# Linear phase: the sums of q's squares beside those of u, and one product of v between the turned scales and their spreading

## The reference

```python
x = x + attention(layernorm(x), wq, wk, wv, wo)
x = x + ffn(layernorm(x), W_r, W_k, W_v, mu_r, mu_k)
x = x + linear(layernorm(x), Wq, Wk, Wv, Wf, Wb, A_log, dt_bias, Wg, bg, Wo, norm_w)
x = x + ffn(layernorm(x), W_r, W_k, W_v, mu_r, mu_k)        # x: (2, 2048, 128) float32

def linear(x, ...):                                        # 16 heads of width 64
    q, k, v = silu(x @ Wq), silu(x @ Wk), silu(x @ Wv)     # each (2, 2048, 16, 64)
    f = sigmoid(x @ Wf - dt_bias);  beta = sigmoid(x @ Wb)
    q, k = l2norm(q), l2norm(k)                            # over the 64 of a head
    for t in tokens:                                       # state: (2, 16, 64, 64)
        o[t] = (q[t] . state) * f[t]
        state = A[head] * state + beta[t] * outer(k[t], v[t])
    o = o * rsqrt(mean(o * o, over the 64) + 1e-5) * norm_w
    return (o * sigmoid(x @ Wg + bg)) @ Wo
```

## Time and profile before

| what | value |
|---|---|
| median of 3 runs | 908.69 us (906.55 to 910.41) |
| the profiled execution | 905.67 us, its span 901.5 us |
| PE busy, share of the span | 814.4 us, 90% |
| DVE, ACT, POOL busy | 556.2, 570.5, 584.7 us (62%, 63%, 65%) |
| mean granted clock of TensorE | 0.981; 1.00 in all of the steps of the linear phase that are read below |
| transfers | 12 GB/s of HBM over the span |

### The profile page before, as it was taken

The page is one execution under the profiler, slowest core; times in us unless marked ns, Lnnn a source line. Parts: engine busy times, 40 slices in busy tenths (PEclk is TensorE's granted clock), DMA queues, the critical chain, the costliest instruction groups (busy, mean ns, idle before and its releaser), DMA issues.

```text
span 901.5 us, 31429 instructions
## 1 busy us (share of the span) xinstructions
PE 814.4 (90%) x13280; PEld 707.7 (79%) x13280; DVE 556.2 (62%) x1296; ACT 570.5 (63%) x1202; POOL 584.7 (65%) x514
## 2 busy tenths in 40 slices
PE   4958998999797799999999999999999999996977
PEld 3647997899696687888788888888888887875866
DVE  3976666566684356567467466567467566567463
ACT  4746554655565666767767767767767767664544
POOL 4983211320445888977977967977977977977332
PEclk9988999999998899999999999999999999999999
DMA  5101000100100000000000000000000000000011
GB/s 188 29 12 36 21 16 1 31 19 2 25 1 1 1 3 3 4 3 3 3 3 3 4 3 3 4 3 3 3 3 3 3 3 3 3 3 3 5 32 58
DMA packets 19417, 12.38 MB, mean 14 GB/s; under 512 B 7760, under 2 KB 18768, under 8 KB 19024
## 3 DMA queue, kind: packets, MB, share of 16 engines
q1 hardware_dynamic: 19280, 10.39, 4.0%
HBM read 8.29 MB, written 2.10 MB: 12 GB/s over the span
## 4 chain that ended last, share of the span: by engine, by line
PE 55%; POOL 4%; DVE 4%; issue 3%; ACT 2%; DVEq 0%; POOLq 0%; ACTq 0%
PE la_ps L1465 9%; PE la_ps L1467 8%; PE la_ps L1466 8%; PE la_o_ps L1528 4%; PE la_o_ps L1544 4%; PE la_s_ps L1558 3%; PE la_ps L1575 3%; PE la_ps L1509 3%; PE la_ps L1496 2%; PE la_ps L1609 2%; PE la_ps L1610 2%; PE la_ps L1611 2%; DVE la_u L1765 1%; POOL la_scale L2141 1%; PE la_ps L1598 1%
## 5 line engine op out<-in xcount | busy, mean ns | idle before, releaser
L2109 POOL TENSOR_TENSOR la_coef<-la_ssk,lt_mhalf 128x32 f32<-128x32 f32 x16 | 87.1, 5442 | 70.2 <-DVE la_ssk L1782 70.2
L1465 PE MATMUL la_ps<-la_x_hi,w_hi 128*128 128x256 f32 x384 | 115.0, 300 | 1.8 <-ACT la_v L1922 1.7
L1467 PE MATMUL la_ps<-la_x_hi,w_lo 128*128 128x256 f32 x384 | 107.5, 280 | 0.4 <-issue 0.4
L1466 PE MATMUL la_ps<-la_x_lo,w_hi 128*128 128x256 f32 x384 | 107.3, 279 | 0.0
L2141 POOL TENSOR_TENSOR la_scale<-la_scale,lt_mhalf 128x32 f32<-128x32 f32 x16 | 99.9, 6241 | 6.8 <-DVE la_scale L1758 6.8
L1805 DVE TENSOR_TENSOR lt_state<-la_s_ps,la_faded 128x512 f32<-128x512 f32 x62 | 42.6, 686 | 70.0 <-PE la_o_ps L1544 57.6
L1465 PEld LDWEIGHTS la_ps<-la_x_hi,w_hi 128*128 128x128 f32 x384 | 72.2, 188 | 11.2 <-issue 6.2
L713 ACT ACTIVATE at_probs<-at_s_ps,at_ntop 128x512 f32<-128x512 f32 (+2 forms) x80 | 49.0, 623 | 46.5 <-DVE at_ntop L655 46.4
L598 PE MATMUL at_o_ps<-V,at_probsT 128*128 128x128 f32 x544 | 74.5, 277 | 3.2 <-DVE at_probsT L507 2.0
L531 POOL CAST at_q_hi<-qk_hi 128x128 fp32r<-128x128 f32 x32 | 9.4, 294 | 104.6 <-PE at_s_ps L572 102.2
L598 PEld LDWEIGHTS at_o_ps<-V,at_probsT 128*128 128x128 f32 x544 | 68.9, 192 | 6.4 <-ACT at_probsT L729 2.3
(11 more groups left out here) (216 smaller groups left out, 2493.6 us busy)
## 6 DMA issues: line engine op xcount, KB each, us to landing
at_w_raw<-in_w SPq DMA_DIRECT2D x20, 128.0 KB, 2.2
X<-in_x SPq DMA_DIRECT2D x8, 256.0 KB, 2.9
out<-X SPq DMA_DIRECT2D x8, 256.0 KB, 2.3
qkv_cos<-in_cos SPq DMA_DIRECT2D x1, 1024.0 KB, 4.8
qkv_sin<-in_sin SPq DMA_DIRECT2D x1, 1024.0 KB, 6.9
lt_w_out<-in_w_out SPq DMA_DIRECT2D x4, 128.0 KB, 2.7
const<-in_const SPq DMA_DIRECT2D x1, 320.5 KB, 3.3
qkv_w<-in_w_qkv SPq DMA_DIRECT2D x1, 320.0 KB, 3.9
```

Of the source, the lines that this page charges most:

```text
L1465: eng.matmul(out, l_hi, r_hi, start=True, stop=False)
L1466: eng.matmul(out, l_hi, r_lo, start=False, stop=False)
L1467: return eng.matmul(out, l_lo, r_hi, start=False, stop=True)
L2109: eng.tensor_tensor(coef[:, :], ssk[:, :], mhalf[:, :], ALU.pow).then_inc(s["coef_step"], 1)
```

## The change

- `square_q` moves from ACT's first half of step m (two instructions of 1024 elements per partition) to the end of q's work in step m - 1, as one instruction of 2048 elements, into a buffer of its own, `la_sq_q`.
- PE sums q's squares directly behind those of u, ahead of `f2`, and no longer behind `k3`. The ring's list changes with it.
- DVE's `guard_q` stands between `add_totals` and `gather_totals`, no longer behind `new_state(m, 0, 0)`.
- `v2` stands on PE between `sB` and `b0`; on ACT its `silu` stands behind `copy_scales`, ahead of the second `square_k`.
- `la_total`, `la_scT` and `la_yT` now share one place in SBUF.

The diff, cut to its core:

```diff
...
         u = sb("u", [P, NP, W])
+        sq_q = sb("sq_q", [P, NP, W])
         with ExitStack() as before_scaling:
...
         ssq = sb("ssq", [P, W])
-        total = sb("total", [P, W])
+        with ExitStack() as before_scales:
+            total = before_scales.enter_context(nc.sbuf_tensor("la_total", [P, W], F32))
+        with ExitStack() as before_output:
+            scT = before_output.enter_context(nc.sbuf_tensor("la_scT", [P, W], F32R))
+        yT = sb("yT", [P, W])
         scale = sb("scale", [P, B, H])
-        scT = sb("scT", [P, W], F32R)
-        yT = sb("yT", [P, W])
...
         LAST = NT - 1
-        ring = Ring(("f0 f1 su f2 sT f3 be k0 k1 v0 v1 kT0 kT1 s10 s11 k2 k3 sq sB b0 b1 b2 b3 v2 v3 q0 q1 q2 q3 y g0 g1 yt g2 "
+        ring = Ring(("f0 f1 su sq f2 sT f3 be k0 k1 v0 v1 kT0 kT1 s10 s11 k2 k3 sB v2 b0 b1 b2 b3 v3 q0 q1 q2 q3 y g0 g1 yt g2 "
                      "kT2 kT3 s00 s01 g3 xt").split(), has, STEPS, BANKS)
...
                         eng.wait_ge(tables.ones_set, 10)
-                    eng.wait_ge(s["qsq_ready"], 2 * (m + 1))
+                    eng.wait_ge(s["qsq_ready"], m + 1)
                 else:
...
                         mm = eng.matmul(ps[bank][32 * quad:32 * (quad + 1), 0:W], pick[:, r if job == "sq" else 2 + r, :],
-                                        sq[:, chunk, :], start=(r == 0), stop=(r == 1))
+                                        (sq_q if job == "sq" else sq)[:, chunk, :], start=(r == 0), stop=(r == 1))
                 mm.then_inc(full[bank], 1)
...
                 if now:
+                    sum_squares(m, "sq")
                     by_feature(m, "f2")
...
                 if now:
-                    sum_squares(m, "sq")
                     recall(m, 0, 1)
...
                     turn_scales(m)
+                if nxt:
+                    by_token(m, "v2")
+                if prv:
                     for j in range(4):
...
                 if nxt:
-                    by_token(m, "v2")
                     by_token(m, "v3")
...
             def guard_q(m):
+                if m > 0:
+                    taken(eng, m, "su")
                 bank = written(eng, m, "sq")
...
                     add_totals(m)
+                if now:
+                    guard_q(m)
+                if prv:
                     gather_totals(m)
...
                     new_state(m, 0, 0)
-                    guard_q(m)
                 if nxt:
...
                     eng.wait_ge(s["qd_second"], m + 1)
-                    eng.wait_ge(s["qsq_ready"], 2 * (m + 1))
+                    eng.wait_ge(s["qsq_ready"], m + 1)
                 bank = written(eng, m, f"q{j}")
...
                 taken(eng, m, f"b{j}")
-                if j == 0 and exists(m):
-                    written(eng, m, "sq")
                 part = slice(2 * j, 2 * j + 2)
...
-            def square_q(m, half):
-                if half == 0 and m > 0:
-                    written(eng, m, "su")
-                part = slice(half * NP // 2, (half + 1) * NP // 2)
-                eng.activation(sq[:, part, :], qT[:, part, :], ACT.Square).then_inc(s["qsq_ready"], 1)
+            def square_q(n):
+
+                taken(eng, n - 1, "q3")
+                if n > 0:
+                    written(eng, n - 1, "sq")
+                eng.activation(sq_q[:, :, :], qT[:, :, :], ACT.Square).then_inc(s["qsq_ready"], 1)
...
                     written(eng, m, "y")
-                elif b == 0:
-                    written(eng, m, "sq")
                 eng.activation(sq[:, :, tile(b)], u[:, :, tile(b)], ACT.Square).then_inc(s["usq_ready"], 1)
...
                     silu_token(m, "k1")
-                if now:
-                    square_q(m, 0)
                 if nxt:
...
                     copy_kT(m, 1)
-                if now:
-                    square_q(m, 1)
                 if nxt:
...
                 if nxt:
+                    silu_token(m, "v2")
                     square_k(m + 1, 1)
...
                     high_u(m, 1)
-                if nxt:
-                    silu_token(m, "v2")
-                if prv:
                     high_u(m, 2)
...
                         silu_q(m, j)
+                    square_q(m + 1)
                 if m == -1:
```

## The result

The changed kernel takes 910.25 us (median of 20 runs, 907.92 to 914.56) against 906.70 us of the kernel before on the same chip (20 runs, 903.71 to 912.65). The ratio is 1.0033, with a 95% interval of 1.0017 to 1.0049: about 3.0 us slower (1.5 to 4.4). That is under the 0.5% (4.5 us) that the prediction took as the bound of a change, and in the range that was forecast, but more than the +0.4 us of the sum.

The account below looks back on a forecast made before the run. PE was taken to bound each step; terms -0.7 - 0.3 + 1.0 - 0.1 + 0.5 = +0.4 us, added to the median of 908.69, forecast 909.1 us, with an 8-in-10 range of 903.8 to 914.3 us.

Parts of the forecast that it names:

- its own case: Whole kernel: no change of size, chance 0.62, with its own range of 905.5 to 912 us.
- v2 in the gap: PE between `sB` and `b0`: filling the gap gains only 0.05 us a step, -0.7 us over 14 steps.
- The wait ahead of `y`: PE before `y`: a new wait for DVE's low part, 0.3 to 0.7 us a step.
- q's squares on ACT: ACT between q's `silu` and `copy_y`: one instruction of about 2.0 us, covered by the existing wait; cost 0.
- `sq` beside `su`: PE, q's sums beside u's: changeover saved, mostly given back waiting for the state; -0.02 us a step, -0.3 in all.
- The reserve of POOL: POOL's power starts 0.97 us later; its 1.0 us reserve before `update` is used up, but no more.
- The last step: Last step: later gathering delays the state PE waits for, +1.0 us, once.
- Step 0: Step 0: `sq` moves from ahead of a `recall` to ahead of a long wait for x, -0.1 us.
- The waits without a cause: PE's thick stretches: idle time with no engine as cause, 13.8 us in 460, grows by +0.5 us in all.
- The rival by which the thick stretch starves: Thick stretch without `sq`: `recall` and `update` wait about 0.35 us more in 14 steps; 913.5 us, chance 0.15.

Follow-up runs that it names:

- e1: Kernel before with only v2 moved between `sB` and `b0`, its silu early on ACT, q's squares as before; ratio to before 0.9994.
- e2: Kernel before with only the q's squares part of the change, v2 left in its old place; ratio to before 1.0036.
- e4: Changed kernel, but in the last step alone `sq` and `guard_q` stand in their old places; ratio to before 1.0006.
- e10: Changed kernel with moments 2 and 3 of the next layer put behind the state in the last step; ratio to before 1.0004.
- e5: Kernel before with v2 moved and `y` waiting for each low part separately, q's squares as before; ratio to before 0.9929.
- e12: Changed kernel with `y` waiting part by part and the next layer's moments behind the last step's state; ratio to before 0.9902, 897.36 us.
- e3: Changed kernel with `y` waiting for each low part by itself instead of for all four; ratio to before 0.9929, 899.22 us.
- e9: Kernel before with moments 2 and 3 of the next layer put behind the state in the last step; ratio to before 0.9951.
- e8: e5 with ACT reordered: v3's silu ahead of the last two high parts, q0's ahead of the last; ratio to before 0.9966.
- e11: e5 with the next layer's moments 2 and 3 behind the last step's state; ratio to before 0.9872, 894.63 us.
- e7: Kernel before with 64 more small instructions on PE (tile 1's beta products repeated), nothing else; ratio to before 0.9994.

## Why the prediction was right or wrong

The time came out in its own case and range, and no rival's mechanism took over. The size did not: +0.4 us was forecast and +3.0 measured, because two small terms of a step and the term of the last step were too low. That 909.1 us lies only 1.2 from the measured 910.25 is luck: the sum started from 908.69 us, the median of three runs, and 20 runs of the kernel before give 906.70. The terms themselves can be read from the starts of PE's instructions. This table is the mean over 13 steps of one profiled execution each, in us, cut at `sB`, at the start of `y`, behind `y`, at the squares of u (with q's where they stand together), behind them, and at the start of the last product of `k3`:

| kernel | `sB` to `y` | `y` | to squares | squares | to last of `k3` | to `sB` |
|---|---|---|---|---|---|---|
| before | 6.57 | 2.87 | 10.87 | 1.00 | 9.85 | 2.98 |
| e1, v2 only | 6.47 | 2.97 | 10.81 | 1.00 | 9.85 | 2.98 |
| e2, squares only | 6.68 | 2.87 | 10.74 | 1.86 | 9.78 | 2.20 |
| after | 6.59 | 2.97 | 10.85 | 1.86 | 9.81 | 2.19 |
| e4 | 6.59 | 2.97 | 10.83 | 1.86 | 9.77 | 2.18 |
| e10 | 6.59 | 2.97 | 10.84 | 1.86 | 9.80 | 2.19 |
| e5, v2 and parts | 6.22 | 2.87 | 10.76 | 1.00 | 9.85 | 2.98 |
| e12 | 6.23 | 2.87 | 10.76 | 1.86 | 9.77 | 2.19 |

- **v2 in the gap: right in its mechanism, and worth nothing.** I forecast -0.05 us a step, since DVE's eight instructions hold `y`. `y` came 0.10 earlier (e1), and the ten hundredths were lost again at once: after a wait, the same products of `y` take 2.97 and not 2.87 us. That restart was not in the sum. e3 and e5 show what held the gain, since with `y` waiting part by part it is 0.35 us a step and stays.
- **The wait ahead of `y`: right, at the low end of the 0.3 to 0.7 forecast.** On the weight loads it is 5.1 us in 13 steps, 0.4 each; from start to start it is 0.33 in the step shown (0.45 less 0.12), though its row names only 0.17. Part of the rest is spent one place earlier, where `q3` starts late: in the step shown it starts at 563.64, just behind v3's `silu`.
- **q's squares on ACT: right.** They are covered; 0.47 us of `copy_y`'s wait is left.
- **`sq` beside `su`: this is the term that was mis-sized**, -0.02 us a step forecast. `su` and `sq` together take 1.86 us, so +0.86; behind `k3`, 2.98 fell to 2.19, so -0.79. The difference is +0.07. The wait of the second `recall` for the state is there (6.9 us in 22 waits, 1.5 in 9 before), and from that `recall` to `update` it is now 0.70 us in most steps and was 0.52, which I had not counted.
- **A step that I left out.** `k3` now ends 0.8 us nearer to `sB`, and with it everything that starts from its result: `silu` and squares on ACT, sum of k's squares and the state on DVE, and only then the scaling. I moved the gathering along DVE's order, but did not follow `k3` down its own chain. DVE had 0.56 us in hand, and the chain came 0.74 later (the state ends at +1.70, before at +0.96). That makes `y` 0.11 to 0.12 later (e2 against before, after against e1): with v2 in the gap by way of the low parts, without it by way of v2's bank. It eats what v2 won in the kernel with both parts.
- **The reserve of POOL: right.** The power waits 11.7 us in 12 steps, and its keys are waited for once.
- **The last step: right in place, too small.** +1.0 forecast, +1.83 measured, +2.34 in e2. The state, which was the whole of the term, comes 0.63 us later (1.13 in e2), and of the clock's part I had nothing: it is 1.20 (1.21 in e2), between the `recall` and `sB`. In the earlier trace rows the `recall` still takes 0.69, after 1.13. e4 and e10 show that the wait for the state is the cause: in the changed kernel with the earlier `guard_q`, or with the moments behind the state, the wait is 2.96 and 2.02 us and not 4.37, the `recall` takes 0.69 again, and the step is 32.54 and 31.67.
- **Step 0: -0.1 forecast, not seen.** From the first product of the phase to the first `sB` it is 69.61 us (282.25 to 351.86), before 69.50 (280.68 to 350.18).
- **The waits without a cause: +0.5 forecast.** The two long columns of the table fell by 0.02 and 0.04 us a step, 0.8 us in 13, and in kernels that share an order they differ by as much (10.83 to 10.85, but 10.74 in e2). No change can be told. The rival by which the thick stretch starves is out: without the 1.00 us of the squares the column to `sB` grew by 0.21, under the 0.3 from which it decides; 0.18 of this is the slower start of `update` behind the wait for the state, and PE's waits without a cause ahead of `recall` fell from 12.1 to 7.8 us. (Its pace of `sq`, a third of the small products', is a quarter by the earlier trace rows: 16 in 1.00 us against 32 in 0.51.)

By these terms: 13 x (0.02 + 0.10 + 0.07 - 0.06) is 1.7 us, and the last step 1.8, together 3.5, with 3.0 (1.5 to 4.4) measured. e1 gives 13 x (-0.10 + 0.10 - 0.06), -0.8, with -0.5 measured.

What stays open is the fine split. e4 leaves 0.5 us of loss (-1.1 to +2.1) where its own profile leaves 0.8 (+1.0 in 13 steps, -0.2 in the last). e10 over e9 is 4.8 us where the terms give 1.7 and 0.8 in the last step: 2.3 us that no term names, a little more than the uncertainty of the ratio. The sum over 13 steps scatters by as much: before and e9, with the same work in the same order, differ there by 2.8 us. That the squares' part costs in the steps is shown by its columns, not by a ratio of its own.

## What to carry to other kernels

When work is taken out from ahead of a point, ask what else is counted from there: whatever is started by the last result before the gap comes nearer to the next deadline by the same time, and its chain must be followed to the end with its reserve. A gap on the busiest engine is worth filling only when the next consumer does not wait for another engine's whole chain; splitting that wait by parts cost two lines and, with v2 in the gap, gave 0.7% (0.3% without it, behind the last `sB`). At the end of a phase, put nothing that can wait ahead of what the last step waits for: there a wait can cost itself and the clock behind it.

## What the runs showed of the hardware

**The clock behind a wait.** Twenty microseconds around the end of the last step, after, e2, e4 and before (length, busy times, clock):

```profile
825.20:845.20 20.00, 12.37 (x117) 11.61 (x118) 10.09 (x31) 5.45 (x10) 8.38 (x10) 0.74 0.00 1
```

```profile
823.26:843.26 20.00, 12.59 (x110) 11.67 (x111) 10.05 (x31) 4.62 (x9) 8.35 (x10) 0.57 0.00 1
```

```profile
821.84:841.84 20.00, 13.38 (x194) 11.81 (x186) 11.63 (x34) 5.58 (x11) 9.57 (x10) 0.83 0.01 2
```

```profile
820.00:840.00 20.00, 13.34 (x194) 11.78 (x186) 11.60 (x33) 6.36 (x12) 9.56 (x10) 0.83 0.01 2
```

PE fell from 2.4 to 1.2 GHz in each; with 4.37 us of standing still ahead of it, in after and e2, it stayed there longer than behind 2.69 and 2.96 us. It is not always the same: after and e2 have the same wait and the same order in this step, and 0.74 and 0.57. So a wait of 1.68 us more came with 1.8 and 2.3 us more of time, of which 1.2 is the lower clock. The length of this wait does not decide alone: in e5 the `recall` takes 0.94 us behind 2.40 us of standing still, in e8 1.13 behind 2.88, and in e4 0.69 behind 2.96. What else decides, no run here shows. In e11, where the `recall` waits 0.59 us and `y` behind it 2.39, the clock is 1.00 from 803 to 843 us.

**The restart.** Behind a wait of 0.2 to 0.4 us PE needs 0.10 us longer for the 24 products of `y` (2.97 and 2.87 in the table), in every kernel that waits there (before, e2, e3, e5 and e12 do not, and show 2.87). It is the first product alone: in the step shown the second starts 0.22 us behind it (564.79 to 565.01), where later ones follow by 0.12.

**Waits that the profile gives no engine for.** e7 moved them between the steps with 64 instructions that have nothing to do with them, while the clock was 1.00, and the time did not change. In kernels with the same number of instructions on PE (before, e1, e9) they cut a `recall` at the same product of the same step, and their length differs (1.21 and 0.49 us at one place). A single step of one profile therefore tells a gain from a loss only beyond 1.5 us between different instruction streams, and beyond 0.7 for the same one; means over many steps, cut into short pieces, repeat to about 0.02 us where the work is not the thick stretches'. What PE waits for there no row shows. That it is the supply of instructions is my reading of the fixed places; if it is, the rule of the Trainium skill that the prediction named (Runtime: NRT & Kernel Launch, instruction fetch mechanics), by which the crossing of a block is mostly hidden, is not borne out in these stretches.
